# Contexts quantised straight into bytes of zeroed fp16 words, with their column sums added up on GpSimd, in a fused cross-attention and LoRA layer

## What is computed

```
def fake_quant(x, scale, zp):
    q = clip(round(x / s + z), 0, 255)
    return (q - z) * s
x = x + matmul(fake_quant(layernorm(x)), fake_quant(ctx_4096))     # x (2,512,1024), ctx (2,1024,1024)
y = layernorm(x)
result = y @ base_w.T + base_b
w = softmax of the top 2 of y @ gate_w.T, 0 for the other 6 experts
result = result + 2 * sum over e of w[e] * (y @ lora_A[e].T) @ lora_B[e].T
x = x + result
```

## Time and profile before

| what | us |
|---|---|
| median of 3 runs | 167.5 |
| the profiled execution: span from first to last instruction | 166.1 |
| PE busy in that span | 159.7 (96%) |
| DVE busy | 111.5 (67%) |
| ACT busy | 83.8 (50%) |
| POOL busy | 29.3 (18%) |
| mean rate of the DMAs | 197 GB/s |

### The profile page before, as it was taken

The page is one execution under the profiler, slowest core; times in us unless marked ns, Lnnn a source line. Parts: engine busy times, 40 slices in busy tenths (PEclk is TensorE's granted clock), DMA queues, the critical chain, the costliest instruction groups (busy, mean ns, idle before and its releaser), DMA issues.

```text
span 166.1 us, 2372 instructions
## 1 busy us (share of the span) xinstructions
PE 159.7 (96%) x824; PEld 121.6 (73%) x824; DVE 111.5 (67%) x258; ACT 83.8 (50%) x111; POOL 29.3 (18%) x65
## 2 busy tenths in 40 slices
PE   5979999999999999999999999999999999999993
PEld 2334444788888878888878688888788888998882
DVE  3976699999999899995785828881380367122051
ACT  3099869957895644273344097175190719200030
POOL 3702042000500402404630040120052000000000
PEclk9999999999999999999999999999999999999999
DMA  5999999979999699204999955959409995000033
GB/s 203 316 417 419 409 409 361 272 238 318 342 230 266 207 197 358 112 0 79 201 161 197 152 117 103 316 157 134 99 5 194 180 249 193 4 0 2 0 126 126
DMA packets 22045, 32.68 MB, mean 197 GB/s; under 512 B 13714, under 2 KB 13970, under 8 KB 22034
## 3 DMA queue, kind: packets, MB, share of 16 engines
q1 hardware_dynamic: 20016, 25.20, 48.1%
q0 software_dynamic: 2016, 7.34, 24.1%
q10 hardware_dynamic: 2, 0.00, 0.0%
HBM read 22.05 MB, written 4.19 MB: 158 GB/s over the span
## 4 chain that ended last, share of the span: by engine, by line
PE 84%; DMA 7%; SPq 3%; ACT 2%; DVE 2%; issue 1%
PE ps_odd L1134 27%; PE ps_even L1134 20%; PE ps_att L1079 11%; DMA ring<-in_ctx 7%; PE ps_g L1115 5%; PE ps_even L1079 2%; PE ps_g L1118 2%; PE ps_t L1058 2%; PE ps_even L1167 2%; PE ps_even L1168 2%; PE ps_even L1169 2%; ACT qc L460 1%; PE ps_odd L1197 1%; PE ps_odd L1196 1%; PE ps_odd L1195 1%; SPq L266 1%
## 5 line engine op out<-in xcount | busy, mean ns | idle before, releaser
L1134 PE MATMUL ps_odd<-w_hi,yt 128*128 128x512 f32 x128 | 38.0, 406 | 0.0
L1079 PE MATMUL ps_att<-c,c1t 128*128 128x512 f16 x96 | 31.3, 383 | 0.5 <-DVE c L735 0.4
L1134 PEld LDWEIGHTS ps_odd<-w_hi,yt 128*128 128x128 f32 x128 | 23.6, 189 | 5.0 <-issue 0.4
L1134 PE MATMUL ps_even<-w_hi,yt 128*128 128x512 f32 x96 | 26.9, 397 | 0.0
L1115 PE MATMUL ps_g<-ag,yt 128*128 128x272 f32 x64 | 21.6, 372 | 0.0
L1134 PEld LDWEIGHTS ps_even<-w_hi,yt 128*128 128x128 f32 x96 | 17.8, 188 | 3.9
L1134 PE MATMUL ps_odd<-w_lo,yt 128*128 128x512 f32 x64 | 19.6, 392 | 0.0
L1134 PE MATMUL ps_even<-w_lo,yt 128*128 128x512 f32 x48 | 15.1, 403 | 0.0
L746 DVE SCALAR_TENSOR_TENSOR x_sb<-ps_att,q_ss,x_sb 128x512 f32<-128x512 f32 x12 | 8.5, 743 | 9.2 <-PE ps_att L1079 8.6
L541 ACT ACTIVATE y_words<-yt_planes 128x1024 uint16<-128x1024 uint16 x8 | 10.3, 1355 | 8.7 <-DMA yt_planes<-y_planes 8.7
L460 ACT ACTIVATE qc<-ring,q_in,q_rec 128x1024 uint16<-128x1024 f32 x11 | 13.6, 1233 | 1.7 <-DMA ring<-in_ctx 1.3
(11 more groups left out here) (150 smaller groups left out, 300.3 us busy)
## 6 DMA issues: line engine op xcount, KB each, us to landing
ring<-in_ctx SPq DMA_DIRECT2D x12, 512.0 KB, 6.7
x_sb<-in_x SPq DMA_DIRECT2D x8, 512.0 KB, 6.6
w_raw<-in_w_t SPq DMA_DIRECT2D x8, 512.0 KB, 16.1
x_sb<-in_base_b POOLq DMA_DIRECT2D x8, 512.0 KB, 7.7
out_x<-x_sb SPq DMA_DIRECT2D x15, 256.0 KB, 2.4
x_sb<-zfix POOLq DMA_DIRECT2D x6, 512.0 KB, 6.5
x_sb<-in_ctx SPq DMA_DIRECT2D x4, 512.0 KB, 8.4
ag_raw<-in_ag_t SPq DMA_DIRECT2D x1, 544.0 KB, 15.1
```

What stands on the lines that cost most here:

```text
L1079: ins = pe.matmul(att_bank(t)[h][:, :], c1t[:, t % 4, k, :], c2[:, k, h * HALF:(h + 1) * HALF], start=(k == 0), stop=(k == CT - 1))
L1134: pe.matmul(ffn_bank[t % 2][h][:, :], rows_of(part, t, k), w[:, k, h * HALF:(h + 1) * HALF], start=start, stop=False)
```

## The change

A context tile takes one step. `scale_context` writes bytes (the conversion to uint8 bounds them to 0 and 255) into the low halves of the words of `c2`, which were zeroed before; such a word read as fp16 is the byte times 2^-24, and the scales take up the factor 2^24 (`WORD_UNIT`). `cut_context`, the slots `qc` and their waits go. `zero_words` fills the eight tiles of `c2` with zeros, three on DVE and five on POOL; the second batch writes bytes over bytes. A context of the second batch now waits in `scale_context` for `att_done` 8 and for the sums of the first batch.

Column sums of both batches are integer adds of 32-bit words (two sums at once) on POOL, seven per batch, each waiting for its context and the add before it. Two matmuls per batch then multiply ones by `csum`; those of the first batch go into `ps_g` and `ps_t` and stand on PE ahead of `attention(2, 0, 0)`. DVE adds attention to tile 0 ahead of the columns. x is centred at its own rounded zero point, kept in a tensor (`less_centre`, `less_word`), which takes four small instructions on DVE. SP loads context 0 ahead of x tile 1, and context 1 ahead of x tile 2.

```diff
             def scale_context(k):
                 act.wait_ge(q_ready, 1)
+                context_free(act, k)
                 context_landed(act, k)
-                if k >= QSLOTS:
-                    act.wait_ge(c2_ready, k - QSLOTS + 1)
-                act.activation(qc[:, k % QSLOTS, :], context_raw(k), ACT.Relu, bias=q_in[:, 3:4],
-                               scale=q_rec[:, 2:3]).then_inc(cact_ready, 1)
+                act.activation(context_bytes(k), context_raw(k), ACT.Relu, bias=q_in[:, 3:4],
+                               scale=q_rec[:, 2:3]).then_inc(c2_in[k % CT], 1)
...
+        def context_free(eng, k):
+            if k < CT:
+                if k in VEC_ZEROED:
+                    eng.wait_ge(vec_zeroed, VEC_ZEROED.index(k) + 1)
+                else:
+                    eng.wait_ge(pool_zeroed, pool_zeroes.index(k) + 1)
             else:
-                eng.wait_ge(cact_ready, act_scaled.index(k) + 1)
+                eng.wait_ge(att_done, 2 * TPB)
+                eng.wait_ge(csum_ready, CT - 1)
...
+            def sum_context(k):
+                i = k % CT
+                a = c2[:, 0, :] if i == 1 else csum[:, :]
+                if i == 1:
+                    context_scaled(pool, k - 1)
+                    if k > CT:
+                        pool.wait_ge(colsum_psum, 1)
+                else:
+                    pool.wait_ge(csum_ready, (CT - 1) * (k // CT) + i - 1)
+                context_scaled(pool, k)
+                pool.tensor_tensor(csum[:, :].bitcast(I32), a.bitcast(I32), c2[:, i, :].bitcast(I32),
+                                   ALU.add).then_inc(csum_ready, 1)
...
             def add_columns():
                 dve.wait_ge(colsum_psum, 1)
-                dve.wait_ge(ss_ready, 1)
-                dve.wait_ge(qx_ready[0], 2)
+                dve.wait_ge(att_taken, 2)
...
-            add_columns()
             x_shift(3)
             add_attention(0)
+            add_columns()
             variance(1, 0)
...
-            def column_sums_first(k):
-                pe.wait_ge(c2_ready, k + 1)
+            def column_sums(b):
+                pe.wait_ge(csum_ready, (CT - 1) * (b + 1))
+                if b == 0:
+                    wait_t_bank()
+                    t_bank_free[0] = (columns_taken, 2)
+                else:
+                    pe.wait_ge(out_ready, 4)
                 for h in range(2):
-                    ins = pe.matmul(ps_even[h][:, :], ones[:, :], c2[:, k, h * HALF:(h + 1) * HALF],
-                                    start=(k == 0), stop=(k == CT - 1))
-                if k == CT - 1:
-                    ins.then_inc(colsum_psum, 1)
+                    ins = pe.matmul(column_bank(b, h)[:, :], ones[:, :], csum[:, h * HALF:(h + 1) * HALF],
+                                    start=True, stop=True)
+                ins.then_inc(colsum_psum, 1)
...
+            def centre_constants():
+                dve.wait_ge(q_taken, 1)
+                chain(dve.tensor_copy(z_byte[:, :], q_in[:, 1:2]))
+                chain(dve.tensor_scalar(less_centre, z_byte[:, :], -1.0, 0.0, ALU.mult, ALU.add))
+                dve.tensor_scalar(d1, q_in[:, 1:2], less_centre, -1.0, ALU.add, ALU.mult).then_inc(centre_ready, 1)
+                dve.tensor_scalar(less_word, less_centre, -BYTE_ONE, 1.0, ALU.add, ALU.mult).then_inc(centre_ready, 1)
...
-            warm_up(2)
+            warm_up(4)
             spread_scales()
-            warm_up(12)
+            warm_up(10)
```

More of the change, by code:

```diff
@@ L12 @@
 U8 = mybir.dt.uint8
+I32 = mybir.dt.int32
 U32 = mybir.dt.uint32
@@ L26 @@
 RING = 4
-QSLOTS = 3
+WORD_UNIT = 2.0 ** 24
+VEC_ZEROED = (0, 1, 2)
 VEC_SCALED = (2, 5)
@@ L192, in xattn_ffn @@
         rowfix_ready = sem("rowfix_ready")
-        cact_ready = sem("cact_ready")
-        cvec_ready = sem("cvec_ready")
-        c2_ready = sem("c2_ready")
+        vec_zeroed = sem("vec_zeroed")
+        pool_zeroed = sem("pool_zeroed")
+        centre_ready = sem("centre_ready")
+        c2_in = [sem(f"c2_in{k}") for k in range(CT)]
         csum_ready = sem("csum_ready")
@@ L227, in xattn_ffn @@
         ss, ssd1, ssd2, ssdd = (q_ss[:, i:i + 1] for i in range(4))
-        act_scaled = [k for k in range(2 * CT) if k not in VEC_SCALED]
+        less_centre, less_word, d1 = (centre[:, i:i + 1] for i in range(3))
+        pool_zeroes = [k for k in range(CT) if k not in VEC_ZEROED]
         def context_raw(k):
@@ L303, in _ @@
             load_x(0)
+            load_context(0)
             load_x(1)
-            load_context(0)
+            load_context(1)
             load_x(2)
-            for k in range(1, 8):
+            for k in range(2, 8):
                 load_context(k)
@@ L380, in scale_product, with zero_words @@
                 pool.wait_ge(q_taken, 1)
-                chain(pool.tensor_scalar(ss, q_in[:, 0:1], q_in[:, 2:3], 1.0, ALU.mult, ALU.mult))
+                chain(pool.tensor_scalar(ss, q_in[:, 0:1], q_in[:, 2:3], WORD_UNIT, ALU.mult, ALU.mult))
+            def zero_words(k):
+                pool.memset(c2[:, k, :].bitcast(F32), 0.0).then_inc(pool_zeroed, 1)
+            def sum_context(k):
[10 more added lines that the diff above has]
+                                   ALU.add).then_inc(csum_ready, 1)
             def x_scale(t):
@@ L414, in add_bias @@
                                accum_op=ALU.add).then_inc(bias_added[t], 16)
+            zero_words(3)
+            zero_words(4)
             scale_product()
             square_constants()
+            x_scale(0)
+            zero_words(5)
+            x_scale(1)
             quant_constants()
-            for k in range(0, 4):
-                x_scale(k)
+            zero_words(6)
+            zero_words(7)
+            x_scale(2)
+            sum_context(1)
+            sum_context(2)
+            sum_context(3)
+            sum_context(4)
+            sum_context(5)
+            x_scale(3)
+            sum_context(6)
+            sum_context(7)
             add_zfix(2)
@@ L674, in quant_reciprocals, with zero_words @@
                 dve.wait_ge(q_taken, 1)
-                chain(dve.reciprocal(q_rec[:, :], q_in[:, :]))
-                dve.tensor_scalar(q_d[:, :], q_in[:, :], -1.0, CENTRE, ALU.mult, ALU.add).then_inc(q_ready, 1)
+                dve.reciprocal(q_rec[:, :], q_in[:, :]).then_inc(q_ready, 1)
+            def centre_constants():
[4 more added lines that the diff above has]
+                dve.tensor_scalar(less_word, less_centre, -BYTE_ONE, 1.0, ALU.add, ALU.mult).then_inc(centre_ready, 1)
+            def zero_words(k):
+                dve.memset(c2[:, k, :].bitcast(F32), 0.0).then_inc(vec_zeroed, 1)
             def variance(ln, t):
@@ L874, in _ @@
             byte_ones(0)
+            zero_words(0)
             byte_ones(1)
+            zero_words(1)
+            zero_words(2)
             take_scales()
```

128 lines of the change are left out of this document (49 added, 79 removed).

## The result

The changed kernel takes 173.72 us (median of 4 runs, 173.51 to 174.07); the kernel before, run beside it, 167.72 us. The ratio is 1.0363, 95% interval 1.0342 to 1.0384: slower by 6.0 us. The span of the profiled execution is 172.1 against 166.1 us, also 6.0 more. The prediction was 171.9 us in a range of 170.0 to 174.0, slower with a chance of 0.94. So the direction and the range hold, and the size is 1.8 us short (0.2 of it is the kernel before, which was on record with 167.5 us). Two disturbed executions (905.5 us in the first experiment, 563.1 us in the seventh) are left out of all that follows.

The account below looks back on a forecast made before the run. PE was taken to bound the kernel from 23 us on, so delays there reach the end: 167.5 + 4.05 (first batch's sums) + 0.35 (second batch's) = 171.9 us, range 170.0 to 174.0.

Parts of the forecast that it names:

- What bounds the kernel, and the fixed points: PE bounds from 23 us on; a shift at tile 3's transposes (24.46 us before) reaches the end unless new waits add.
- the second batch's part: At the second batch's column-sum matmuls PE waits for POOL's seven adds, ending at 75.0 instead of 74.69 us: +0.35 us.
- The waits: PE waits 3.4 us for POOL's last first-batch add, then about 2 us for `scale_x(3)` before tile 3's transposes.
- The price of an add: One 512-word add on POOL, worked out from memset and cast rows: 1.22 us, following each other every 1.30 us.
- The rival of cheaper adds: POOL's adds take 0.86 us (total 170.8 us) or 0.5 us (170.1 us); chance 0.15.
- The lock of the shared ports: DVE's context 5 pass would hold up POOL's adds, 172.5 us; forecast rejected it; rival's chance 0.10, shared with dearer adds.
- the 21.18 us of the sum: Predicted start of POOL's `x_scale(3)`, after five adds ending at 21.0 us and the variance DVE starts at 19.55 us.
- From the pair to the transposes: From the first batch's two sum matmuls to tile 3's transposes, the order and time of before were taken as unchanged.
- the predicted 4.05: First batch's shift: its two sum matmuls end at 25.35 instead of 21.30 us, moving tile 3's transposes to 28.5 us.
- The clock: Rival: after idling 3.4 and 2 us for the first batch's sums, PE falls to half rate: +1.2, 173.1 us; chance 0.10.
- Nothing for the zeroes, the centring and the cuts: Zeroing words and four centring instructions hide before data arrives; dropped cuts gain only 0.43 us between ACT and `c2`.
- The loads: x tile 1, now third, lands at 8.04 us; `x_scale(2)` ends about 14.5 us, five adds behind it; tile 3 unchanged.

Follow-up runs that it names:

- the first experiment: Changed kernel with the first batch's column sums back as sixteen matmuls on PE; 170.1 to 171.3 us in three executions, ratio 1.0175 to the kernel before.
- experiment 7: Changed kernel with first-batch sums back on PE, second-batch adds back on DVE and the loads in the order of before; 167.84 us, ratio 1.0007.
- experiment 2: Changed kernel with the second batch's seven adds back on DVE, in fp16 and in the places of before; 172.57 us, ratio 1.0313.
- experiment 6: Changed kernel with first-batch sums back on PE and second-batch adds back on DVE, the changed load order kept; 169.72 us, ratio 1.0103.
- experiment 5: Changed kernel with eleven keep-warm matmuls in place of three ahead of the transposes of tile 0; 174.66 us, ratio 1.0432.
- experiment 4: Changed kernel with SP's loads back in the order of the kernel before, the sums left on POOL; 173.42 us, ratio 1.0343.

## Why the prediction was right, and where its sizes were off

**What bounds the kernel, and the fixed points:** right. PE's idle time from 23 us on and the shift of two fixed points account for the whole result, 4.46 + 1.45 of 6.0 us, and experiments 1, 2, 6 and 7 take the result apart along these lines, back to no difference. Of the 1.8 us that the forecast is short, the first batch has 0.4 and the second 1.1. No rival had the second batch's part: that the result still lies in the range, 0.3 us below its end, is in part luck.

**The waits:** right in place, order and cause. The pair waits for the last add (2.83 us, 3.4 predicted; PE got there at 22.6 instead of 21.3 us; about 0.3 us of that is its half clock until about 17 us, by experiment 5, where it got there at 21.87 us with all else 0.45 us earlier), then PE waits for `scale_x(3)` behind `zfix` (1.58, about 2 predicted), then it is dense.

**The price of an add:** right. 1.22 us was worked out from a memset and a cast, and 1.26 measured. The rival of cheaper adds falls.

**The lock of the shared ports: the step that failed.** The prediction said "The rows say that it won't: a pass into uint8 takes 0.55 us for 512 elements, but one into uint16 0.80 us for 1024, so the new pass (about 1.1 us) is not in the faster form". It takes 0.81 us, as the one into uint16 did, and the add beside it 1.80. The 0.55 us was a poor guide: the cost of such a pass does not grow in proportion to its elements (0.55 us for 512, 0.81 for 1024). The rule that stood beside it (the Trainium skill, SBUF — State Buffer, Who interferes with whom) was right, and its 172.5 us nearer than 171.9, though it was given 0.8 us of lock where 0.5 came. The trace agrees with the rule's other half too, that DVE instructions with two inputs in SBUF and a POOL instruction that reads SBUF hold each other up: `x_shift` at 0.21 us became 1.22. The shift of `x_scale(3)` from the 21.18 us of the sum to 21.84 is made of this: 0.53 us of lock, 0.15 of cadence (1.34 instead of 1.30) and 0.18 from a later start, 0.86 in all, of which the sum had 0.2 of slack. The later start has a pass beside it too, the one over context 2 at 13.50 us: the second half of `x_scale(2)` took 0.96 instead of 0.55 us there. No experiment took that pass away, so this is argued from the overlap. The trace of before has the same, beside its pass at 12.77 us:

```profile
12.81 0.79 POOL L388 TENSOR_TENSOR qa<-r_v,minus_half 128x1 f32<-128x1 f32 x1
```

**From the pair to the transposes** 3.75 us were taken over from before (20.71 to 24.46), and 3.48 came (25.44 to 28.92). Before, `scale_x(3)` had also waited for `x_shift(3)`, which stood behind `add_columns` on DVE; this wait is gone. Together: 0.66, 0.03 more from `x_scale(3)` to the pair (3.60 instead of 3.57), less 0.27, is 0.4 us over the predicted 4.05.

**The second batch was mis-sized:** 1.45 instead of 0.35 us. Its seven adds end at 72.33 + 8.21 = 80.54 us; by the prediction, 75.0 and the shift of 4.46, at 79.46. They start 0.5 us late, mainly because `x_scale(5)` met DVE's pass over y at 69.38 us (its first half took 0.80 instead of 0.34 us), and seven take 9.57 us where 9.02 were reckoned. The wait was reckoned with adds and an x scale that no work of DVE meets, although the row of 1.23 us at 66.87 is this same `x_scale(5)` before the change. Two slips of addition change little: the steps listed give 65.00 where the prediction has 64.95, and 12.0 for the variance of tile 2 where it has 11.8 (it came at 11.70).

**The clock:** the rival expected a fall after the waits for the sums. In the changed kernel there was none (1.00 from 23 to 60 us); it fell earlier, after PE's waits of 2.04 and 1.41 us for tile 0, which the prediction had put in its steps (a quantisation at 9.8 us instead of 7.26) without asking what PE does meanwhile. Three matmuls at 13.59 us took 1.49 instead of 0.81 us. By experiment 5 that was hidden behind POOL (17.64 us from x tile 1 to the pair at either clock). Experiment 4 has the fall where the rival put it. The Trainium skill (TensorE: Matmul & The Clock Gate, The HAM clock gate) says that an idle TensorE falls to the lower rate; both places agree, with the numbers given, and the wait of 2.83 us shows that not every wait brings it down.

**Nothing for the zeroes, the centring and the cuts:** right (experiment 7, 1.0007). **The loads:** the prediction let them act through POOL alone. Through PE they cost 1.9 us once POOL's adds are gone.

## What to carry to other kernels

Work taken from the bounding engine is worth what the next engine's chain leaves: here 3.1 us of matmuls went, and seven dependent adds of 1.34 us on a slow engine, two of them behind a late x scale, put 4.4 us of waits in their place. Cost a step on POOL with its DVE neighbours in the same stretch, in both directions: here a pass of 0.81 us added 0.5 to a chain of adds, and the adds made a DVE instruction of 0.21 us take 1.2. An earlier start (loads, warm-up) reaches the end only through the chain that arrives last, so test it together with the edit that changes which chain that is. And before a small difference between two executions is put down to an edit, look at when the loads landed in each.

## What the runs showed of the hardware that had not been expected

- A pass of DVE from fp32 into every second byte takes 0.81 us for 1024 elements, no more than one into uint16 (0.80), while one for 512 takes 0.55.
- An integer add of 128x512 words on POOL takes 1.26 us and follows a dependent one after 1.34 to 1.38 us; where DVE's byte pass had begun first, it took 1.80, and where the add had begun first, the pass took 1.34 instead of 0.81 (experiment 4).
- A one-element-per-partition instruction of DVE took 1.21 to 1.24 us, six times its usual 0.21, because an add of POOL was running; in the kernels without that add it took 0.21 to 0.22.
- After waits of 2.04 and 1.41 us, with four transposes between them, PE ran at half rate until about 17 us; after 1.37 and 1.41 us around the same transposes (experiment 4) it did not, nor after one of 2.83 us behind a dense stretch; after one of 3.67 us it did, until about 28.7 us. Four executions of one kernel had mean clocks from 1.00 to 0.969 and differed by 2.25 us.
